# Weights' preparation of a four-layer cross-attention kernel: fold products in alternating row halves, copies and splits on other engines

## The reference, cut to what matters

```python
q = x @ Wq; k = ctx @ Wk; v = ctx @ Wv            # 16 heads of 64
logits = (q_h @ k_h.T) * 64 ** -0.5 + col_bias     # -20 at two token pairs where a mask is 0
x = softmax(logits) @ v_h @ Wo + bo + x
```

## Time and profile before

| | us |
|---|---|
| median of 3 runs | 1819.43 (1819.06 to 1823.53) |
| the profiled execution | 1819.92 |
| its span, first to last instruction | 1817.5 |
| first instruction of TensorE's main part (L1274) | 57.82 |

### The profile page before, as it was taken

The page is one execution under the profiler, slowest core; times in us unless marked ns, Lnnn a source line. Parts: engine busy times, 40 slices in busy tenths (PEclk is TensorE's granted clock), DMA queues, the critical chain, the costliest instruction groups (busy, mean ns, idle before and its releaser), DMA issues.

```text
span 1817.5 us, 72896 instructions
## 1 busy us (share of the span) xinstructions
PE 1760.4 (97%) x28400; PEld 1510.9 (83%) x28400; DVE 1578.3 (87%) x3010; ACT 1471.7 (81%) x2987; POOL 1599.4 (88%) x2136
## 2 busy tenths in 40 slices
PE   6599999999999999999999999999999999999996
PEld 6478888888888888888888888888888888888885
DVE  6689988899889998899888998899888898889983
ACT  4388888888888888888888888888888888888873
POOL 3389999999999999999999998999999999999973
PEclk7599999999999999999999999999999999999998
DMA  5269999999999999999999999998999999999996
GB/s 173 43 134 191 174 181 191 186 185 170 192 185 184 183 171 186 193 179 185 176 187 189 177 187 180 187 188 171 189 183 186 183 174 183 178 170 188 174 186 130
DMA packets 1168210, 320.35 MB, mean 176 GB/s; under 512 B 1140246, under 2 KB 1164124, under 8 KB 1167868
## 3 DMA queue, kind: packets, MB, share of 16 engines
q1 hardware_dynamic: 1167868, 315.69, 94.0%
HBM read 15.93 MB, written 4.19 MB: 11 GB/s over the span
## 4 chain that ended last, share of the span: by engine, by line
PE 90%; issue 1%; DMA 1%; SPq 1%; ACT 0%; DVE 0%; ACTq 0%; DVEq 0%
PE ring L1226 50%; PE sc L1368 12%; PE o_ps L1226 9%; PE o_ps L1386 5%; PE ring L1440 5%; PE sc L1347 4%; PE ring L1297 2%; PE sc L1366 1%; PE ring L1421 1%; PE ring L1437 1%; DMA arena<-p_sm 1%; PE ring L1274 0%; PE o_ps L1382 0%; PE ring L1277 0%; SPq L485 0%
## 5 line engine op out<-in xcount | busy, mean ns | idle before, releaser
L1226 PE MATMUL ring<-ctx_four,m_w 128*128 128x154 f16 x6144 | 461.4, 230 | 1.5 <-ACT o_tf L710 0.9
L1226 PEld LDWEIGHTS ring<-ctx_four,m_w 128*128 128x128 f16 x6144 | 428.8, 96 | 2.5 <-ACT o_tf L710 1.3
L1107 DVE TENSOR_TENSOR arena<-sc,row_max 128x616 f32<-128x616 f32 (+1 forms) x384 | 387.0, 1008 | 7.0
L644 POOL TENSOR_TENSOR p_sm<-arena,p_sm 128x616 f16<-128x616 f32 x256 | 334.6, 1318 | 39.5 <-ACT p_sm L710 38.0
L639 POOL TENSOR_TENSOR p_sg<-arena,p_sg 128x512 f16<-128x512 f32 (+1 forms) x256 | 341.9, 1357 | 2.3 <-ACT p_sg L710 2.3
L710 ACT ACTIVATE arena<-ring 128x462 f16<-128x462 f32 (+1 forms) x384 | 198.9, 518 | 153.9 <-PE ring L1226 153.5
L1086 DVE TENSOR_TENSOR arena<-ring,arena 128x462 f16<-128x462 f32 (+1 forms) x384 | 224.6, 586 | 73.2 <-ACT arena L710 64.2
L1226 PE MATMUL ring<-wv_m,ctx_four 128*103 128x512 f16 (+1 forms) x1152 | 281.1, 380 | 0.9 <-ACT v_all L710 0.9
L671 POOL TENSOR_TENSOR arena<-arena 128x1024 f16<-128x1024 f32 x128 | 272.8, 2131 | 9.3 <-ACT arena L710 9.3
L1368 PE MATMUL sc<-arena,x_s 128*128 128x512 f16 (+1 forms) x1152 | 263.6, 338 | 0.0
L1104 DVE TENSOR_REDUCE row_max<-sc 128x6 f32<-128x462 f32 (+2 forms) x384 | 210.9, 576 | 12.1 <-PE sc L1368 11.5
(11 more groups left out here) (172 smaller groups left out, 3682.0 us busy)
## 6 DMA issues: line engine op xcount, KB each, us to landing
v_fourth<-v_tile SPq DMA_DIRECT2D x64, 105.6 KB
ctx_nat<-in_ctx_dram SPq DMA_DIRECT2D x64, 77.0 KB
x_nat<-in_x_dram SPq DMA_DIRECT2D x64, 64.0 KB, 2.4
arena<-p_sg SPq DMA_TRANSPOSE x256, 3.5
arena<-p_sm SPq DMA_TRANSPOSE x256, 4.4
out_dram<-y_out SPq DMA_DIRECT2D x64, 64.0 KB, 2.2
v_fourth<-v_tile SPq DMA_DIRECT2D x32, 101.6 KB
arena<-in_L_xattn_Wk_dram SPq DMA_DIRECT2D x2, 1024.0 KB, 6.0
```

The costliest lines, as they stand in the source:

```text
L644: pool.tensor_tensor(p_sm[:, k, LO, :, 0:S], probs_m[:, hs, :], p_sm[:, k, HI, :, 0:S], ALU.subtract).then_inc(sems["pm_lo"], 1)
L1107: dve.tensor_tensor(out, s_view[:, hs, :], row_max[:, hs].unsqueeze(2).to_broadcast([P, hs.stop - hs.start, S]), ALU.subtract).then_inc(do ...
L1226: ins = pe.matmul(out, a, b, start=(n == 0), stop=(n == len(passes) - 1))
```

## The change

1. TensorE forms the fold products in the order of `FOLD_ORDER` = 0, 4, 1, 5, 2, 6, 3, 7, two groups at a time, product by product in turn: one from rows 0 to 63, one from rows 64 to 127, in two banks. ScalarE waits for both groups of a pair.
2. The second set of transposed blocks is copied by ScalarE (`turned_weights` with `high(..., 1.0)`).
3. The second `Wv` and `Wo` have staging tiles and a semaphore of their own; `vo_free` and SyncE's wait on it are gone.
4. The high parts of layers 0 and 2 go from ScalarE to GpSimd (`spread_weights`), behind a wait for the two scalings of L1050.
5. The low parts of the first `Wv` and `Wo` go from VectorE to GpSimd (`low_first_out`): a scaling in place and a subtraction for each.
6. VectorE's order is new; GpSimd's four `iota` come first and have a semaphore of their own (`counted`), so `selectors` and `pieces` stand ahead of the small loads. The scalings of L1050 no longer wait for each other. The part of `selectors` from L976 on is now `mask_rows`.

```diff
+        st_wv1 = in_arena(KC * INNER, F32).rearrange("p (k n) -> p k n", k=KC)
+        st_wo1 = in_arena(NOC * D, F32).rearrange("p (k n) -> p k n", k=NOC)
...
+        FOLD_ORDER = [c for pair in zip(range(NMM // 2), range(NMM // 2, NMM)) for c in pair]
...
-                if n:
-                    sp.wait_ge(vo_free, 2)
-                sp.dma_start(st_wv, mha_w[n]["Wv"].rearrange("(k p) n -> p k n", p=P)).then_inc(load_vo, 16)
-                sp.dma_start(st_wo, mha_w[n]["Wo"].rearrange("(k p) n -> p k n", p=P)).then_inc(load_vo, 16)
+                sp.dma_start(st_v[n], mha_w[n]["Wv"].rearrange("(k p) n -> p k n", p=P)).then_inc(load_vo[n], 16)
+                sp.dma_start(st_o[n], mha_w[n]["Wo"].rearrange("(k p) n -> p k n", p=P)).then_inc(load_vo[n], 16)
...
+            def spread_weights():
+
+                pool.wait_ge(scaled_q, 2)
+                for n in range(2):
+                    pool.tensor_scalar(gq_s[:, n, HI], st_gq[:, n, :], W_GQA, None, ALU.mult).then_inc(split_gqa, 1)
+                    pool.tensor_scalar(gk_s[:, n, HI], st_gk[:, n], W_GQA, None, ALU.mult).then_inc(split_gqa, 1)
+                    pool.tensor_scalar(wo_g[n][:, HI], st_go[:, n, :], W_V, None, ALU.mult).then_inc(split_gqa, 1)
+                    pool.tensor_scalar(wv_g[n][:, HI, :, 0:KVG * GD], st_gv[:, n, :, :], W_V, None, ALU.mult).then_inc(split_gqa, 1)
+                    pool.tensor_scalar(wv_g[n][:, HI, :, KVG * GD:], st_gv[:, n, :, 0:(VGROUPS - KVG) * GD], W_V, None, ALU.mult).then_inc(split_gqa, 1)
+                for n in range(2):
+                    for r in range(R):
+                        pool.tensor_scalar(wq_r[n][:, HI, r], st_gq[:, n, :].rearrange("p (g r a d) -> p r g a d", g=KVG, r=R, a=1)[:, r].to_broadcast([P, KVG, 4, GD]),
+                                           W_GQA, None, ALU.mult).then_inc(wide_gqa, 1)
+                    for kc in range(KC):
+                        pool.tensor_scalar(wk_r[n][:, HI, kc], st_gk[:, n, kc, :].rearrange("p (g a d) -> p g a d", g=KVG, a=1).to_broadcast([P, KVG, 4, GD]),
+                                           W_GQA, None, ALU.mult).then_inc(wide_gqa, 1)
+
+            def low_first_out():
+
+                pool.wait_ge(split_vo, 2)
+                pool.tensor_scalar(st_wv, st_wv, W_V, None, ALU.mult).then_inc(pool_step, 1)
+                pool.tensor_scalar(st_wo, st_wo, W_V, None, ALU.mult).then_inc(pool_step, 1)
+                pool.wait_ge(pool_step, 8)
+                pool.tensor_tensor(wv_m[0][:, LO], st_wv, wv_m[0][:, HI], ALU.subtract).then_inc(vo_split, 1)
+                pool.tensor_tensor(wo_m[0][:, LO], st_wo, wo_m[0][:, HI], ALU.subtract).then_inc(vo_split, 1)
...
+            turned_weights()
             split_out(1)
             fold_high(1)
...
-            turned_weights(0)
-            dve.wait_ge(consts_pool, CONSTS)
+            turned_weights()
+            dve.wait_ge(counted, 4)
+            selectors()
+            pieces()
             dve.wait_ge(load_small, 16 * SMALL_LOADS)
...
             fold_low(0)
...
+            mask_rows()
+            dve.wait_ge(scaled_q, 2)
+            split_gqa_weights()
+            dve.wait_ge(consts_pool, CONSTS)
             bias_factors()
...
+            split_out()
+            fold_low(1)
...
+                k = n * PREP + NTQ + NTK
+                for i in range(0, NMM, 2):
                     for m in range(4):
...
+                        for t in range(2):
+                            place, kc = divmod(FOLD_ORDER[i + t] * 4 + m, KC)
+                            r, pair = place // NOC * MD, place % NOC
+                            ins = pe.matmul(prep_banks[(k + t) % NB][:, m * P:(m + 1) * P], wk_t[r:r + MD, pair, kc * P:(kc + 1) * P],
+                                            wq_t[r:r + MD, pair, :], start=True, stop=True)
+                            if m == 3:
+                                ins.then_inc(prep_raw, 1)
+                    k += 2
```

More of the change, by code:

```diff
@@ L300, in build @@
         gk_s = in_arena(4 * KC * KVG * GD, F16).rearrange("p (n a k d) -> p n a k d", n=2, a=2, k=KC)
+        st_wv1 = in_arena(KC * INNER, F32).rearrange("p (k n) -> p k n", k=KC)
+        st_wo1 = in_arena(NOC * D, F32).rearrange("p (k n) -> p k n", k=NOC)
+        st_v, st_o = [st_wv, st_wv1], [st_wo, st_wo1]
         mask_r = in_arena(8 * P, F32)[0:6].rearrange("p (n t) -> p n t", n=8)
@@ L398, in build @@
         load_qk = sem("load_qk")
-        load_vo = sem("load_vo")
-        vo_free = sem("vo_free")
+        load_vo = [sem(f"load_vo{n}") for n in range(2)]
+        vo_split = sem("vo_split")
         consts_pool = sem("consts_pool")
@@ L409, in build @@
         prep_hi = sem("prep_hi")
-        prep_free = sem("prep_free")
+        turned_first = sem("turned_first")
+        turned_second = sem("turned_second")
+        fold_free = sem("fold_free")
+        scaled_q = sem("scaled_q")
+        wide_gqa = sem("wide_gqa")
+        counted = sem("counted")
         prep_banks = [t[:, n, :] for t, size in ((ring, RING), (o_ps, 2), (sc, 3)) for n in range(size)]
@@ L567, in _ @@
                                pattern=[[-1, P]], channel_multiplier=1).then_inc(ident_ready, 1)
+            pool.iota(part_i[:, :], pattern=[[0, 1]], base=0, channel_multiplier=1).then_inc(counted, 1)
+            pool.iota(key_i[:, :], pattern=[[1, S]], base=0, channel_multiplier=0).then_inc(counted, 1)
+            pool.iota(flat_i[:, :], pattern=[[P, BLOCKS]], base=0, channel_multiplier=1).then_inc(counted, 1)
+            pool.iota(head_i[:, :], pattern=[[S, H + 1]], base=0, channel_multiplier=0).then_inc(counted, 1)
             pool.memset(ones[:, :], 1.0).then_inc(consts_pool, 1)
@@ L570, in _ @@
             pool.memset(minus_half[:, :], -0.5).then_inc(consts_pool, 1)
[L571 to L574, removed]
             pool.memset(bias_l[:, :], 0.0).then_inc(consts_pool, 1)
@@ L599, in _ @@
             pool.wait_ge(load_small, 16 * SMALL_LOADS)
+            def spread_weights():
[20 more added lines that the diff above has]
+                pool.tensor_tensor(wo_m[0][:, LO], st_wo, wo_m[0][:, HI], ALU.subtract).then_inc(vo_split, 1)
+            spread_weights()
+            low_first_out()
             def x_parts(it, j):
@@ L712, in split_out @@
             def split_out(n):
-                act.wait_ge(load_vo, 32 * (n + 1))
-                high(wv_m[n][:, HI], st_wv, W_V).then_inc(split_vo, 1)
-                high(wo_m[n][:, HI], st_wo, W_V).then_inc(split_vo, 1)
+                act.wait_ge(load_vo[n], 32)
+                high(wv_m[n][:, HI], st_v[n], W_V).then_inc(split_vo, 1)
+                high(wo_m[n][:, HI], st_o[n], W_V).then_inc(split_vo, 1)
             def fold_high(n):
-                for c in range(NMM):
-                    k = n * PREP + NTQ + NTK + c
+                for i, c in enumerate(FOLD_ORDER):
+                    k = n * PREP + NTQ + NTK + i
+                    act.wait_ge(prep_raw, k + 1 + (i + 1) % 2)
+                    high(m_w[n][:, HI].rearrange("p h k c -> p (h k c)")[:, c * BANK:(c + 1) * BANK], prep_banks[k % NB], W_M).then_inc(prep_hi, 1)
@@ L722, in fold_high, with turned_weights @@
+            def turned_weights():
+                for c in range(NTQ + NTK):
+                    k = PREP + c
                     act.wait_ge(prep_raw, k + 1)
-                    high(m_w[n][:, HI].rearrange("p h k c -> p (h k c)")[:, c * BANK:(c + 1) * BANK], prep_banks[k % NB], W_M).then_inc(prep_hi, 1)
+                    dst = (wq_t if c < NTQ else wk_t).rearrange("p a b -> p (a b)")
+                    o = (c if c < NTQ else c - NTQ) * BANK
+                    high(dst[:, o:o + BANK], prep_banks[k % NB], 1.0).then_inc(turned_second, 1)
@@ L937, in step, with turned_weights, split_out @@
                 dve.wait_ge(dve_step, steps[0])
-            def turned_weights(n):
+            def turned_weights():
                 for c in range(NTQ + NTK):
-                    k = n * PREP + c
-                    dve.wait_ge(prep_raw, k + 1)
+                    dve.wait_ge(prep_raw, c + 1)
                     dst = (wq_t if c < NTQ else wk_t).rearrange("p a b -> p (a b)")
                     o = (c if c < NTQ else c - NTQ) * BANK
-                    dve.tensor_copy(dst[:, o:o + BANK], prep_banks[k % NB]).then_inc(prep_free, 1)
+                    dve.tensor_copy(dst[:, o:o + BANK], prep_banks[c % NB]).then_inc(turned_first, 1)
             def fold_low(n):
-                for c in range(NMM):
-                    k = n * PREP + NTQ + NTK + c
-                    dve.wait_ge(prep_hi, n * NMM + c + 1)
+                for i, c in enumerate(FOLD_ORDER):
+                    k = n * PREP + NTQ + NTK + i
+                    dve.wait_ge(prep_hi, n * NMM + i + 1)
                     part = slice(c * BANK, (c + 1) * BANK)
                     low(m_w[n][:, LO].rearrange("p h k c -> p (h k c)")[:, part], prep_banks[k % NB], W_M,
[L955 to L961, removed]
```

(61 more changed lines are left out.)

## The result

| | before | after |
|---|---|---|
| median of 11 runs each, us | 1819.67 (1818.51 to 1823.53) | 1824.39 (1822.70 to 1826.27) |
| profiled execution, its span | 1819.92, 1817.5 | 1822.70, 1820.6 |
| first instruction of TensorE's main part | 57.82 | 60.07 |

The ratio is 1.0023, interval 1.0015 to 1.0031. The change makes the kernel slower by 0.23%, less than the 0.3% named above; the forecast was 9.4 us faster.

What follows compares the result with a forecast made beforehand. The prediction took VectorE's serial list in the preparation as what TensorE waits for. Copies (3.59), low parts (3.34) and idle time (2.45) leaving it gave 9.4 us: 1819.9 to 1810.5, as median 1810.0; range 1808.5 to 1825.

Steps and rivals of the forecast that it cites:

- the 0.3% named above: Smallest difference a measurement of this kernel can tell from no change, 5.5 us: faster below 1814.0, slower above 1824.9.
- the sum itself: VectorE's preparation list added part by part: TensorE's main part starts at 48.4 instead of 57.8 us, 9.4 us gained.
- Rival 1: Preparation: VectorE and GpSimd take turns on SBUF tiles; full stall 1822.8 to 1826.2, chance 0.23; partial 1813 to 1819, 0.25.
- the full stall: VectorE waits out GpSimd's instructions in mask_rows, split_gqa_weights and bias_factors: start at 61 to 64 us, chance 0.23.
- the undisturbed sum: Preparation with VectorE's parts at their old lengths: 1810.0 us, own range 1808.5 to 1813, chance 0.40.
- both engines' 90% in the main part: VectorE and GpSimd both about 90% busy at once in the main part, cited as evidence against their taking turns.
- 16 us (13 with short scalings): Forecast VectorE stall in the preparation, if let in only after each GpSimd instruction; depends on the length of the scalings.
- The scalings: GpSimd's in-place scalings of Wv and Wo in the preparation: 4.2 and 2.2 us, taken at 1.9 ns an element.
- Rival 2: Preparation: GpSimd becomes the bound, ending at 49 to 55 us; time 1810.6 to 1817, chance 0.08.
- With no overlap ... 3.9 us late: First fold products: without row halves running at once, the last high part ends at 25.6 and the low part at 26.3.
- Rival 3: First fold products: the alternation of row halves overlaps nothing, 3.9 us late, 1813.9 us; chance 0.04.
- The second products: Second fold products end at 39.5 us (45.5 worst), hidden behind bias_factors with 2 us left in the worst case.

Runs made afterwards that it cites:

- e7: The changed kernel measured again, nothing altered: 1822.52 us against 1819.95 before, ratio 1.0015.
- e4b: Kernel of e3 plus twelve useless GpSimd memsets (writes only) that the main part waits for: 1828.09 us against 1819.95 before, one execution.
- e8: Kernel of e4b with the twelve memsets replaced by copies of a tile onto itself (reads and writes): 1830.05 us against 1819.91 before, one execution.
- e6: Kernel of e3, bias_factors earlier, its casts and copies and first Wv scaling on ScalarE, that Wv's subtraction on GpSimd: 1808.26 us against 1819.95; again 1809.06 against 1819.91.
- e2: Changed kernel with part 4 undone (22 small splits back on ScalarE): 1821.91 us against 1820.52 before, ratio 1.0009.
- e1: Changed kernel with part 5 undone (first Wv and Wo low parts back on VectorE): 1815.70 us against 1820.52 before, ratio 0.9970.
- e3: Changed kernel with parts 4 and 5 undone, GpSimd idle from 15.5 us to the main part: 1814.33 us against 1820.52 before, ratio 0.9963.
- e5: Kernel of e3 with the fold groups in their old order 0 to 7, still pairwise into two banks: 1813.33 us against 1819.95 before, one execution.

## Why the prediction was wrong, step by step

**The step that failed** is the sum itself: it priced VectorE's parts from rows in which GpSimd stood still, and kept them when GpSimd was given work beside them. The terms that failed are `split_gqa_weights`, 3.28 us in the sum and 8.27 measured, and `bias_factors`, 8.57 and 14.78. The sum said 1810.0 with a start at 48.4; it was 1824.4 and 60.07. Rival 1 had this mechanism and its place. It worked out 1822.8 to 1826.2, from a start 3.4 to 6.8 us later, and 1824.4 came, with a start only 2.25 us later: that the time fell into the rival's range is in part luck, for with the +2.57 of e7 it would have been 1822.2. My stated range, 1808.5 to 1825, holds 1824.4 only because it was drawn over this rival. I gave the full stall 0.23 and the undisturbed sum 0.40. The rows could not decide, and I let both engines' 90% in the main part speak against it, though the same sentence said that the inputs there are of another kind. In the trace of the kernel before, each of VectorE's 22 costliest groups after 60 us has an input in PSUM (`sc`, `ring` or `o_ps`), so that 90% said nothing of instructions on SBUF alone. `fold_low` beside a busy GpSimd in e4b, e8 and e6 shows that such an input keeps an instruction from being held.

**The rule.** What the Trainium skill (SBUF — State Buffer, § Who interferes with whom) states agrees with the runs at most points tried: two SBUF inputs beside reads wait (e8, 1.60 us for 0.15), beside pure writes they do not (e4b, 0.15), copies and scalar instructions in a fast form wait for either, an input in PSUM waits for neither. The page also says that the wait lasts for the whole instruction. In most places it did (e2: 5.30 against 5.36 us). Beside in-place scalings it did not always: `wo_g` was let go at 33.82 us with L629 running until 35.40, and the first L1045 kept its 0.24 us at 37.02 with L630 running until 38.15. Nor was every short scalar instruction held: the comparisons L1023 of 77 elements took 0.25 to 0.31 us each beside GpSimd's wide splits (the pair at 27.91 us took 0.54, with L620 running from 27.50 to 28.64), while in e4b the same comparisons waited up to 1.6 us for a `memset`. No run here shows why.

**The stall's size.** I had 16 us (13 with short scalings), measured were 11.4. Too many instructions were counted as held: the twelve wide splits were to cost up to 0.54 each and all 22 splits together cost VectorE 0.43 (e1 against e3), and after `wo_g` several low parts passed freely.

**The scalings** of 2048 and 1024 elements took 5.41 and 2.78 us, not 4.2 and 2.2: 2.6 ns an element, not the 1.9 that I took from the two-input rows. They lay within the bounds (2.4 to 8.6). GpSimd ended at 45.0, forecast 42.0. Rival 2, GpSimd as the bound, did not occur: VectorE released TensorE.

**The fold products.** That two row halves run at once was right, as read from the 0.05 us in the earlier trace rows: the first sixteen records (eight products) of both halves took 1.16 us where the kernel before took 2.05, and e5, with two banks but one row half at a time, also 2.05. "With no overlap ... 3.9 us late" was wrong: it assumed clock 0.50, and the clock stayed at 1.00 (e5). Rival 3 would have had no price in that execution.

**The second products** were hidden as forecast: TensorE had idled 29.3 us when it was released.

**The rest.** The parts of VectorE's list were right to 0.2 us over 34 us (e3, 51.90 against 51.7), and so was the claim that the time follows the start.

## What to carry to other kernels

When work moves to GpSimd to relieve VectorE, look at what VectorE does in that stretch, not at how busy GpSimd is: instructions with an input in PSUM go on undisturbed (e6), those on SBUF tiles can wait out GpSimd's instruction, however short they are (17 elements, 5.30 us). A few long GpSimd instructions were worse than many short ones: four of 2.7 to 5.4 us cost 11.1 us, 22 of 0.3 to 0.6 us cost 0.4. That is not a clean comparison, for the first ten short ones ran beside `fold_low(0)` and the rest mostly beside `mask_rows`, and it is open why the comparisons there were not held. If the path of a serial list of small instructions has to get shorter, an idle ScalarE is the safe place, even where its instruction is slower (a bias copy of 1232 elements takes it 1.2 us and VectorE 0.5).

## What the runs showed that I had not expected

- GpSimd's `tensor_scalar` in place costs 2.6 ns an element (5.36 and 5.41 us for 2048), more than its two-input subtraction, 2.0 ns (4.06 us for 2048).
- A `memset`, which reads nothing, holds VectorE's comparisons of 77 elements up: in e4b eight of them averaged 1.55 us for 0.25, beside `memset`s of 1.83 us.
- TensorE's granted clock fell to 0.50 at 15.7 us in the kernel before, with TensorE busy since 13.3 us, and only after 27 us in e5, when TensorE had stood nearly still since 24 us (0.14 us busy in 4). e5 forms the same first products, pairwise into two banks. Why its clock held through them is open.
